# Bringing the softmax shift from columns into rows: a TensorE transpose through the bank ring and 4 row transfers, in place of a VectorE transpose and 8 transfers

## The reference, cut to what matters

```python
# x: (4, 1024, 256); 16 query heads, 4 key/value heads, head size 16
q = rope(x @ wq); k = rope(x @ wk); v = x @ wv
scores = einsum('bqkgd,bskd->bkgqs', q, k) / sqrt(16)
attn = softmax(scores, axis=-1)                  # over 1024 keys
out = einsum('bkgqs,bskd->bqkgd', attn, v) @ wo
x = layernorm(x + out)
g, u = x @ Wg.T, x @ Wu.T                        # int32 weights, dequantized
x = layernorm(x + (silu(g) * u) @ Wd.T)
```

## Time and profile before

| | us |
|---|---|
| median of 3 runs | 937.14 |
| lowest, highest of them | 926.76, 939.69 |
| the profiled execution's own time | 939.69 |
| its span, first to last instruction | 937.8 |
| granted TensorE clock, mean | 0.973 |

### The profile page before, as it was taken

The page is one execution under the profiler, slowest core; times in us unless marked ns, Lnnn a source line. Parts: engine busy times, 40 slices in busy tenths (PEclk is TensorE's granted clock), DMA queues, the critical chain, the costliest instruction groups (busy, mean ns, idle before and its releaser), DMA issues.

```text
span 937.8 us, 15836 instructions
## 1 busy us (share of the span) xinstructions
PE 914.1 (97%) x5542; PEld 459.9 (49%) x5542; DVE 752.9 (80%) x1551; ACT 716.2 (76%) x932; POOL 249.3 (27%) x214
## 2 busy tenths in 40 slices
PE   9998899999999999999999999999999999999996
PEld 3323343334334334334334434333334888888885
DVE  5667789999999999999999999999973466655545
ACT  2345678999999999999999999999887555555564
POOL 6653566001001001001000100400101666656455
PEclk9976789999999999999999999999999999999998
DMA  8975524131222213313133222331110201101001
GB/s 252 280 202 162 122 69 112 46 74 42 67 71 69 49 46 91 69 43 74 51 66 67 64 51 55 90 60 44 32 52 14 70 23 45 46 23 46 23 23 47
DMA packets 52641, 68.79 MB, mean 73 GB/s; under 512 B 17104, under 2 KB 26320, under 8 KB 52560
## 3 DMA queue, kind: packets, MB, share of 16 engines
q1 hardware_dynamic: 51696, 64.60, 26.8%
q0 software_dynamic: 864, 3.15, 1.1%
HBM read 46.74 MB, written 16.25 MB: 67 GB/s over the span
## 4 chain that ended last, share of the span: by engine, by line
PE 89%; DVE 4%; DMA 2%; SPq 2%; ACT 2%; issue 1%; POOL 0%; POOLq 0%; DVEq 0%
PE pv_bank L1270 26%; PE ring_bank L1184 25%; PE pair_bank L1328 13%; PE pair_bank L1387 11%; PE pv_bank L1413 3%; PE ring_bank L1413 3%; PE pair_bank L1218 2%; PE ring_bank L1280 2%; SPq L361 1%; DMA q_sb<-shift 1%; ACT probs L1098 1%; DVE block_max L760 1%; PE ring_bank L1295 1%; PE ring_bank L1233 1%; PE pv_bank L1166 1%
## 5 line engine op out<-in xcount | busy, mean ns | idle before, releaser
L1098 ACT ACTIVATE probs<-pair_bank 128x1024 f32<-128x1024 f32 x512 | 495.8, 1024 | 60.5 <-PE pair_bank L1328 58.9
L760 DVE TENSOR_REDUCE block_max<-ring_bank 128x1 f32<-128x512 f32 x732 | 472.4, 684 | 39.8 <-PE ring_bank L1184 30.5
L1184 PE MATMUL ring_bank<-k_max,q_sb 48*128 48x512 f32 x1004 | 314.7, 481 | 8.7 <-DMA q_sb<-shift 4.9
L1184 PEld LDWEIGHTS ring_bank<-k_max,q_sb 48*128 48x128 f32 x1004 | 136.6, 187 | 289.0 <-DVE block_max L760 159.3
L1270 PE MATMUL pv_bank<-probs,v_all 128*17 128x512 f32 x2048 | 273.0, 605 | 0.7 <-ACT probs L1098 0.6
L1328 PE MATMUL pair_bank<-q_sb,k_sb 50*128 50x512 f32 x1024 | 198.4, 416 | 0.7 <-ACT probs L1098 0.5
L617 POOL TENSOR_TENSOR attn<-attn,inv_rows 128x1024 f32<-128x1024 f32 x7 | 16.7, 2383 | 490.5 <-DMA inv_rows<-inv_d 490.5
L955 DVE SCALAR_TENSOR_TENSOR hid<-pair_bank,up_s,silu 128x512 f32<-128x512 f32 x63 | 47.1, 748 | 84.7 <-ACT silu L1145 84.7
L1328 PEld LDWEIGHTS pair_bank<-q_sb,k_sb 50*128 50x128 f32 x1024 | 100.8, 189 | 23.9 <-ACT probs L1098 6.4
L665 POOL TENSOR_TENSOR hid_l<-hid,hid_h 128x512 fp32r<-128x512 f32 x63 | 81.7, 1296 | 86.1 <-ACT hid_h L1124 85.4
L757 DVE CUSTOM_DVE_ANT_0 above<-ring_bank,above 128x512 f32<-128x512 f32 x138 | 95.1, 691 | 9.6 <-PE ring_bank L1184 5.4
(11 more groups left out here) (139 smaller groups left out, 857.5 us busy)
## 6 DMA issues: line engine op xcount, KB each, us to landing
k_max<-k_parts SPq DMA_DIRECT2D x96, 96.0 KB, 3.5
q_sb<-q_parts SPq DMA_DIRECT2D x64, 128.0 KB, 3.1
k_sb<-k_parts SPq DMA_DIRECT2D x96, 64.0 KB, 2.3
attn<-xT SPq DMA_DIRECT2D x8, 512.0 KB, 4.9
q_parts<-high SPq DMA_DIRECT2D x16, 256.0 KB, 3.7
q_parts<-low SPq DMA_DIRECT2D x16, 256.0 KB, 4.0
q_sb<-q_parts SPq DMA_DIRECT2D x64, 64.0 KB, 3.2
q_sb<-shift SPq DMA_DIRECT2D x256, 2.0 KB
```

The costliest lines, as they stand in the source:

```text
L760: dve.reduce_max(block_max[half % 2][:, col:col + 1], bank, axis=AX.X).then_inc(ring_used, 1)
L1098: act.activation(probs[t % 2][:, 2 * pr:2 * pr + 2, :], pair_bank[pr][:], ACT.Exp, scale=D ** -0.5).then_inc(probs_ready, 1)
L1184: pe.matmul(bank, q_sb[k][rows, i, qt * P:(qt + 1) * P], k_max[k // QH][rows, kind * CH:(kind + 1) * CH], start=True, stop=True).then_inc( ...
```

## The change

`row_max` is now transposed by TensorE. `transpose_max(half)` writes 16 partitions x 128 columns into a bank of the ring, as an entry of its own ("split") that has its place between entries 0 and 1 of step t = 5 (SPLIT_AT). VectorE's `split_shift` reads that bank twice: a copy that rounds (the high part), then, after a wait for that copy, a subtraction (the low part), which also frees the bank. `shift_high`, `shift_low`, `turn_shift` and their tiles go. `load_shift` waits for the subtraction (through `ring_used`) and issues 4 DMAs, each of 8 pieces of 128 floats into one row of `q_sb`, in place of 8 DMAs of 16 pieces of 32 floats. For half 0, "split" is placed one step earlier than the three instructions were. The first output projection waits for the last "split" in place of the last maximum; it stays at t = 6.

```diff
-SQ = 32
-SHIFTS = 16 * SHIFT * P // SQ
+SHIFTS = 16 * GROUPS * SHIFT
-HIGH_AT = 4
-OUT_AT = 6
+SPLIT_AT = 5
...
-        shift_rows = [sb(f"shift_rows{c}", [P, SHIFT, G * QT], f32r, two) for c in range(2)]
-        shift = [sb(f"shift{c}", [P, SQ], fp32, two) for c in range(2)]
+        shift = [sb(f"shift{c}", [G * QT, SHIFT, P], f32r, two) for c in range(2)]
...
+            if i == 2 * KT + 1:
+                where.append((0, "split"))
...
+                if e == 1 and split_at(g) is not None:
+                    place((split_at(g), "split"), "max")
...
-            def load_shift(pair, k):
-                sp.wait_ge(shift_ready, HALVES * pair + k + 1)
-                for o in range(SHIFT):
-                    for b in range(P // SQ):
-                        dst = q_sb[k][ROWS + o::GROUP].rearrange("r j (q b p) -> r (j q) b p", q=QT, p=SQ)[:, :, b, :]
-                        src = shift[k % 2][b * SQ + o * G * QT:b * SQ + (o + 1) * G * QT]
-                        sp.dma_start(dst.bitcast(fp32), src).then_inc(shift_loaded[k], 16)
+            def load_shift(pair, k, split):
+                sp.wait_ge(*split)
+                for r in range(GROUPS):
+                    heads = G // GROUPS * QT
+                    for o in range(SHIFT):
+                        row = r * GROUP + ROWS + o
+                        dst = q_sb[k][row:row + 1].rearrange("o j (q p) -> o (j q) p", p=P)
+                        sp.dma_start(dst.bitcast(fp32), shift[k % 2][r * heads:(r + 1) * heads, o, :].bitcast(fp32)).then_inc(shift_loaded[k], 16)
...
-            def shift_high(half):
-                dve.wait_ge(row_max_ready, half + 1)
-                dve.tensor_copy(shift_rows[half % 2][:, 0, :], row_max[half % 2][:]).then_inc(shift_h_ready, 1)
-
-            def shift_low(half):
-                dve.wait_ge(shift_h_ready, half + 1)
-                dve.tensor_tensor(shift_rows[half % 2][:, 1, :], row_max[half % 2][:], shift_rows[half % 2][:, 0, :].bitcast(fp32), ALU.subtract).then_inc(shift_l_ready, 1)
-
-            def turn_shift(half):
-                dve.wait_ge(shift_l_ready, half + 1)
-                if half > 1:
-                    dve.wait_ge(shift_loaded[(half - 2) % HALVES], SHIFTS * ((half - 2) // HALVES + 1))
-                dve.transpose(shift[half % 2][:], shift_rows[half % 2][:].rearrange("p o n -> p (o n)").bitcast(fp32)).then_inc(shift_ready, 1)
+            def split_shift(bank, half, index, guard):
+                if guard is not None:
+                    dve.wait_ge(*guard)
+                dve.tensor_copy(shift[half % 2][:, 0, :], bank[0:G * QT, 0:P]).then_inc(shift_h_ready, 1)
+                dve.wait_ge(shift_h_ready, index + 1)
+                dve.tensor_tensor(shift[half % 2][:, 1, :], bank[0:G * QT, 0:P], shift[half % 2][:, 0, :].bitcast(fp32), ALU.subtract).then_inc(ring_used, 1)
...
+            def transpose_max(half):
+                pe.wait_ge(row_max_ready, half + 1)
+                bank = free_bank((half, "split"))
+                pe.transpose(bank[0:G * QT, 0:P], row_max[half % 2][:], ident[:]).then_inc(ring_ready, 1)
...
                         if t not in MIXED:
+                            if split_at(g) is not None:
+                                transpose_max(split_at(g))
                             maxima(1)
                             maxima(2)
                             scores(0)
...
-                            if k == QH and t == OUT_AT:
-                                pe.wait_ge(*taken_through((HALVES * PAIRS - 1, MAXES - 1)))
-                            part = g - (KT * (HALVES * PAIRS - 2) + OUT_AT)
+                            if k == QH and t == SPLIT_AT + 1:
+                                pe.wait_ge(*taken_through((HALVES * PAIRS - 1, "split")))
+                            part = g - (KT * (HALVES * PAIRS - 2) + SPLIT_AT + 1)
```

More of the change, by code:

```diff
@@ L247, in layer @@
                 for key in early[n, h]:
-                    place(key, key[0] if key[0] in ("v", "gap") else ("above" if blocks(key[0], key[1] // 4)[key[1] % 4][1] == 2 else "max"))
+                    place(key, key[0] if key[0] in ("v", "gap") else "max" if key[1] == "split" else ("above" if blocks(key[0], key[1] // 4)[key[1] % 4][1] == 2 else "max"))
         early_entries = len(readers)
@@ L254, in maxima_at, with split_at @@
             return (half, t) if half < HALVES * PAIRS else None
-        def shift_at(g):
+        def split_at(g):
             n, t = divmod(g, KT)
-            return n + 1 if t == HIGH_AT and n + 1 < HALVES * PAIRS else None
+            return n + 1 if t == SPLIT_AT and n + 1 < HALVES * PAIRS else None
         for g in range(HALVES * PAIRS * KT):
             for e in range(4):
+                if e == 1 and split_at(g) is not None:
+                    place((split_at(g), "split"), "max")
                 if maxima_at(g):
@@ L407, in projections @@
                     if last and c == 1:
-                        load_shift(0, 0)
+                        load_shift(0, 0, taken_through((0, "split")))
                     store_q(m, 1)
@@ L487, in attention @@
                     if k < HALVES - 1:
-                        load_shift(p, k + 1)
+                        load_shift(p, k + 1, taken_through((n + 1, "split")))
                     elif not last:
-                        load_shift(p + 1, 0)
+                        load_shift(p + 1, 0, taken_through((n + 1, "split")))
                     if k % QH == 0 and not last:
@@ L796, in early_maxima @@
                     half, e = key
+                    if e == "split":
+                        split_shift(entry(key), 0, 0, None)
+                        continue
                     take_max(half, e)
@@ L799, in early_maxima @@
                         row_maxima(half)
[L800 to L805, removed]
             for m in range(BLOCKS):
@@ L827, in maxima @@
             def maxima(g):
-                turned, before = shift_at(g), shift_at(g - 1) if g else None
                 for e in range(4):
[L830 to L835, removed]
+                    if e == 1 and split_at(g) is not None:
+                        half = split_at(g)
+                        guard = None if half < 2 else (shift_loaded[(half - 2) % HALVES], SHIFTS * ((half - 2) // HALVES + 1))
+                        split_shift(entry((half, "split")), half, half, guard)
                     if maxima_at(g):
@@ L1050, in early_takes @@
                         gap_high(key[1])
-                    elif key[1] % 4 < 2:
+                    elif key[1] != "split" and key[1] % 4 < 2:
                         difference(key[0], key[1] // 4, (key[1] % 4,))
@@ L1207, in early_work @@
                         make_gap(key[1])
+                    elif key[1] == "split":
+                        transpose_max(key[0])
                     else:
```

3 lines of the change are left out of this document (2 added, 1 removed).

## The result

The changed kernel is slower, by 0.9%. Over 20 runs each its median is 935.24 us (932.26 to 939.65), that of the kernel before 927.22 us (922.01 to 939.69); the ratio is 1.0091, with a 95% interval of 1.0066 to 1.0114. Ratio and interval are of fast runs, without the five runs of before that lie over 1.5% above its fastest; with all 20 of each the means differ by 5.9 us, 0.6%. The times of the changed kernel also scatter less, by 2.3 us (standard deviation) against 5.9. The first three runs of before, from which I predicted, had a median of 937.14: two of the three, and the profiled one, were among the slowest that this kernel has. The profiled execution of the changed kernel took 934.67 us, with a span of 932.8 and a mean clock of 0.984.

What follows compares the result with a forecast made beforehand. The prediction took a TensorE-ScalarE loop, 19.39 us a half, as setting the pace, with VectorE and transfers hidden. Gains of 10.4 against a loss of 9.0 gave -1.4 on the median 937.14: 935.7 us, range 924 to 946.

Steps and rivals of the forecast that it cites:

- The signs named for it: Steady row_max period from 19.39 to about 19.7; scores of t = 5 about 0.3 us later behind the same pv.
- Gains 6.7 + 0.8 + 0.7 + 2.2 = 10.4: Sum of the stalls expected to go, in us: half 2, attention's start, near its end, and stretched VectorE copies.
- start, half 0 to 1: At the attention's start TensorE's 1.57 us wait for the shift goes; 0.8 us counted (bounds 0 and 1.57).
- wait at half 1, half 1 to 2: TensorE's 2.59 us shift wait and the lowered clock behind it go: 6.7 us gained (bounds 0 and 7.2).
- stretched copies, half 2 to 4: VectorE's small copies beside GpSimd go, new PSUM reads are not stretched: 2.2 us back (bounds 0 and 2.2).
- half 29 to the end: Near the attention's end TensorE's 0.72 us wait for the shift goes whole, counted as 0.7 us.
- loss, 30 halves: Transpose and bank wait in the steady loop cost 0.30 us a half, 9.0 us in all (3.6 to 18).
- The issues: SyncE's four shift transfers take 2.2 us to issue, 0.55 each, so the last goes out 2.2 us sooner.
- (a): Entry 2 waits for VectorE's read of entry 0, weight load exposed: 0.60 us a half, +7.6, 944.7 us; chance 0.30.
- (c): Half 2's collision stays, as GpSimd's loads come as much earlier: 6.7 us not gained, 942.4 us; chance 0.10.
- (b): TensorE absorbs the transpose at 0.12 us a half: -6.8, 930.3 us; chance 0.20.
- (d): Four single-partition transfers land over 2 us later after issue, every half waits at t = 0: about 951 us; chance 0.03.

Runs made afterwards that it cites:

- the profile with span 921.2: The kernel before, unchanged, profiled again in the first of three repeats; median 926.64 us, ratio 0.9984.
- three of its variants with four transfers: Changed kernel with one more VectorE 16x128 copy (ratio 1.0083), with the transpose behind the scores (1.0189), or behind entry 3 (1.0149).

## Why the prediction was wrong

**The size of the loss was near.** The forecast had 0.30 us a half and a steady period of 19.7; it is 0.34 and 19.73. From half 4 to 29 that makes 493.33 - 484.83 = 8.5 us, and the medians differ by 8.0. The signs named for it came: the scores of t = 5 start 0.21 us later behind the same pv, and the exponentials 0.49. That it meets ScalarE's and TensorE's loop in full holds, and so does that VectorE's share is covered (0.03 and 0.05 us for 0.27). The price of a VectorE instruction, 0.28, was 0.27 and 0.28. The split of the 0.30 into two terms was wrong: I added 0.15 for the transpose and 0.15 for the bank. The runs show 0.20 for the transpose alone and 0.33 for the bank with hardly a transpose, and the two together give the larger one, not 0.53. The sum came out near by luck.

**What failed is the step "Gains 6.7 + 0.8 + 0.7 + 2.2 = 10.4".** It took the stalls of one execution as the kernel's. Term by term, taken from the times of `row_max` against the changed kernel's profile, with 0.34 us added back for each half of the stretch that pays the loss:

| term, us | forecast | against the first profile of before | against the profile with span 921.2 |
|---|---|---|---|
| start, half 0 to 1 | 0.8 | 1.83 | 0.27 |
| wait at half 1, half 1 to 2 | 6.7 | 7.22 | 0.64 |
| stretched copies, half 2 to 4 | 2.2 | 2.23 | 0.30 |
| half 29 to the end | 0.7 | 0.74 | 0.65 |
| gains together | 10.4 | 12.0 | 1.9 |
| loss, 30 halves | 9.0 | 10.2 | 10.2 |
| balance | -1.4 | -1.8 | +8.3 |

For the execution that was profiled the balance was nearly right, and every term but the start's. For one without the stalls the gains are 1.9 us in place of 10.4, and the balance, +8.3, is what the medians show (+8.0). The two stalls that made up most of the forecast gain stand at full size in two of four profiled executions of before, in one there is a small one of the second sort, and in one they are absent: there half 0 to 4 took 83.19 us, and in the changed kernel 83.00, where three dearer halves are included. Of the 20 times of before 12 lie under 930 us and 8 above 932, so the median is that of an execution with few stalls or none. The mechanisms were seen rightly as far as the changed kernel's own profile shows, which has neither stall; but three of its variants with four transfers have the wait for the shift again (0.66 to 2.46 us at half 1). The highest time of the changed kernel, 939.65, is about that of before, 939.69.

**The number.** The forecast of 935.7 us lies 0.5 from the measured 935.24, and that is luck: it started from a median of 937.14 where 20 runs give 927.22, and it went down by 1.4 where the change goes up by 8.0. The first error is 9.9 us, the second 9.4, and they cancel. The prediction said that "in an execution without it the change would lose 5 us", and took the other case although the lowest of the three times shown, 926.76, asked for an explanation. The third run could have been read as an execution without these stalls: 927 plus 9 is 936, and slower.

**The start and the end.** At the start the wait of 1.56 us for the shift is gone, and one of 0.96 us for ScalarE's relu has come in its place, as I had feared for both engines. Near the end the wait of 0.72 went as well, and what it gave paid for the last two dearer halves: from half 29 on it is 285.27 us against 285.24.

**The issues.** Four were to take 2.2 us and be out by 107.2, 2.2 after the first. They take mostly 2.7 to 2.9, as a single one takes 0.63 us and not 0.55.

**A name.** The prediction speaks of a wait "before half 2". Counted from 0 it is the wait at t = 0 of half 1, in the period that ends with `row_max` of half 2.

**The rivals.** (a), the bank wait, named the right mechanism and the right side, with 0.60 in place of 0.34, and its threshold, 0.35 us against gains of 10.4, was useless as the gains were not there. (c) was right in its premise: the weight load did come earlier with the shift, 2.26 us after the first of the transfers in place of 2.61 to 4.49, and still ahead of the end of the issues. In the changed kernel's profile no wait comes of it; in those of three of its variants one does. (b) and (d) did not come about.

**Still open.** Why the projections of one kernel end anywhere from 67.94 to 74.41 us was not looked into. The seven profiles with the change in them lie between 70.3 and 73.0, the seven without between 67.9 and 74.4; their means are 71.3 and 71.2, so nothing here says that the change makes them longer or shorter. How often the changed kernel has the wait at half 1 is not known from one profile. A ring of four banks, or a place in an even step, was not tried.

## What to carry to other kernels

Before a stall in a profile is counted as a gain, hold the profiled time against the fastest run, and profile the kernel a second time: if the gap is as large as the stall, the stall may be a matter of luck, and what remains for sure is what the change adds in each iteration. In a ring of few banks filled by an in-order engine, an added entry can cost the wait for the entry that then stands one ring length ahead. Its own work beside that wait was free here, and cutting the work saved nothing. A hand-off over many small transfers got dearer here with their number, at the same bytes in all.

## What the runs showed of the hardware

The small copies and subtractions of VectorE from SBUF to SBUF were often held up beside a GpSimd instruction: 16 columns took 1.95 us in place of 0.165. The transpose L778, also from SBUF to SBUF, never was (213 ns at most), nor were the new ones that read PSUM: 269 to 280 ns. Only 8 of those 64 ran beside a GpSimd instruction in the changed kernel, but over the seven profiles with the change it is 78, none over 280 ns. The Trainium skill, "SBUF — State Buffer", section "SBUF: two separate sides", describes the pair of ports that VectorE and GpSimd share as an exclusive lock, held for a whole instruction. The trace agrees where GpSimd subtracts, with the 1.95 us that end when GpSimd's instruction ends. Beside L595, GpSimd's conversion from int32, it does not: in the first profile of before that starts at 101.26 and lasts 2.79 us, and the copy L768, begun at 101.35, ends at 102.34, 1.7 us ahead of it.

What follows from such a stretch was not foreseen. In the run with VectorE's copy TensorE waited 0.97 us for VectorE's reads of the banks, the granted clock was 0.78 from 160 to 165 us and 0.54 from 165 to 170, and the half in which a subtraction of 16 columns was held up took 4.7 us more than its neighbours.
